# Attention products with the values in pairs of groups, four buffers of probabilities, score operands in three slots

## The reference

```python
q = x @ Wq.T + bq;  k, v = jnp.split(x @ Wkv.T + bkv, 2, axis=-1)
dots = jnp.einsum('bhid,bhjd->bhij', q * scale, k)
dots = jnp.where(causal, MASK_VAL, dots)
attn = jax.nn.softmax(dots, axis=-1)
out = jnp.einsum('bhij,bhjd->bhid', attn, v)
...
x = x + 0.5 * _L0_ffn_ref(_layernorm(x), ...)
x = x + _L0_attn_ref(_layernorm(x), ...)
x = x + 0.5 * _L0_ffn_ref(_layernorm(x), ...)
```

## Time and profile before

| | us |
|---|---|
| median of 3 runs | 1394.63 (1393.09 to 1396.85) |
| the profiled execution, its own time | 1394.48 |
| its span in the trace | 1392.7 |
| TensorE busy | 1265.0 |
| VectorE busy | 1095.3 |
| ScalarE busy | 941.5 |
| GpSimd busy | 397.6 |

### The profile page before, as it was taken

How to read it: one execution, slowest core, us unless ns; L and a number is a source line. 1 busy time by engine, 2 the same in 40 slices (tenths; PEclk the granted TensorE clock), 3 DMA queues, 4 the chain that set the end, 5 groups by cost and what they waited for, 6 DMA issues and landing times.

```text
span 1392.7 us, 24439 instructions
## 1 busy us (share of the span) xinstructions
PE 1265.0 (91%) x8356; PEld 547.7 (39%) x8356; DVE 1095.3 (79%) x3527; ACT 941.5 (68%) x1697; POOL 397.6 (29%) x508
## 2 busy tenths in 40 slices
PE   3879999999999999999999999999999999998973
PEld 2323334443344433443344433444344533433332
DVE  5788888778888888878887788878888788779643
ACT  2257776777767677767767777676777677666661
POOL 3223322332323322232323232233223323221120
PEclk9899999999999999999999999999999999999897
DMA  4480433542425433244435423154342234330000
GB/s 139 90 169 13 69 69 57 99 86 56 72 36 99 89 68 69 47 80 84 69 58 99 97 53 71 28 99 96 61 69 56 51 73 69 68 58 31 1 16 19
DMA packets 57832, 95.17 MB, mean 68 GB/s; under 512 B 8352, under 2 KB 51488, under 8 KB 51744
## 3 DMA queue, kind: packets, MB, share of 16 engines
q1 hardware_dynamic: 55664, 92.30, 35.1%
q10 hardware_dynamic: 2032, 1.19, 0.3%
HBM read 59.91 MB, written 33.55 MB: 67 GB/s over the span
## 4 chain that ended last, share of the span: by engine, by line
PE 59%; DVE 17%; ACT 12%; issue 5%; POOL 3%; DVEq 2%; DMA 2%; SPq 1%; POOLq 0%; ACTq 0%
PE o_bank L1225 15%; PE s L1206 13%; PE st L1191 11%; PE misc L1141 7%; ACT q_stack L796 5%; DVE s L953 5%; ACT probs L809 5%; PE misc L1167 4%; PE misc L1136 4%; DVE max_full L957 3%; PE misc L497 3%; POOL probs L682 1%; DVE o_tok L1043 1%; DVE stats L464 1%; PE misc L488 1%
## 5 line engine op out<-in xcount | busy, mean ns | idle before, releaser
L809 ACT ACTIVATE probs<-st 128x512 f32<-128x512 f32 (+1 forms) x1216 | 633.3, 582 | 199.8 <-PE st L1191 109.2
L953 DVE CUSTOM_DVE_ANT_0 s<-s,causal 128x128 f32<-128x128 f32 (+3 forms) x1024 | 494.8, 502 | 140.9 <-PE s L1206 138.1
L1206 PE MATMUL s<-k_stack,q_stack 96*128 96x512 bf16 (+3 forms) x1536 | 490.9, 332 | 38.3 <-DVE max_full L957 12.2
L1191 PE MATMUL st<-q_stack,k_stack 108*128 108x512 bf16 (+3 forms) x1536 | 485.7, 329 | 24.2 <-ACT probs L809 21.6
L957 DVE TENSOR_REDUCE max_full<-s 128x1 f32<-128x512 f32 x512 | 350.0, 684 | 30.8 <-PE s L1206 29.4
L1225 PE MATMUL o_bank<-probs,v_aug 128*17 128x512 f32 (+3 forms) x3072 | 325.7, 496 | 8.8 <-POOL probs L682 6.5
L682 POOL TENSOR_SCALAR_AFFINE_SELECT probs<-probs 128x512 f32<-128x512 f32 x256 | 163.7, 644 | 535.0 <-ACT probs L809 534.8
L1206 PEld LDWEIGHTS s<-k_stack,q_stack 96*128 96x128 bf16 x1536 | 148.9, 98 | 394.8 <-DVE max_diag L953 178.1
L1191 PEld LDWEIGHTS st<-q_stack,k_stack 108*128 108x128 bf16 x1536 | 149.3, 98 | 145.3 <-ACT probs L809 54.9
L694 POOL TENSOR_TENSOR qk<-qk,parts 128x512 f32<-128x512 f32 x64 | 74.2, 1159 | 318.4 <-ACT parts L769 318.4
L953 DVE DVE_READ_ACCUMULATOR2_ANT max_diag<- 128x1 f32 x1024 | 144.8, 141 | 0.0
(11 more groups left out here) (107 smaller groups left out, 859.9 us busy)
## 6 DMA issues: line engine op xcount, KB each, us to landing
part_dram<-parts SPq DMA_DIRECT2D x128, 192.0 KB, 2.8
k_stack<-part_dram SPq DMA_DIRECT2D x186, 128.0 KB, 7.0
q_stack<-part_dram SPq DMA_DIRECT2D x31, 384.0 KB, 5.0
x_all<-x SPq DMA_DIRECT2D x16, 512.0 KB, 10.6
q_stack<-part_dram SPq DMA_DIRECT2D x31, 256.0 KB, 7.4
out<-x_all SPq DMA_DIRECT2D x7, 1024.0 KB, 11.1
q_stack<-part_dram SPq DMA_DIRECT2D x33, 128.0 KB, 8.8
k_stack<-part_dram SPq DMA_DIRECT2D x12, 64.0 KB, 2.9
```

Of the source, the lines that this page charges most:

```text
L809: nc.scalar.activation(probs[:, g % 2, h - part:h + 1, 0:width], st_bank[i % 3][:, 0:share * width] .rearrange("p (h c) -> p h c", c=width ...
L953: nc.vector.tensor_tensor_reduce(out=bank, in0=bank, in1=causal[:, CW - width:CW], scale=1.0, scalar=-BIG, op0=ALU.add, op1=ALU.max, accum ...
L1191: score = nc.tensor.matmul(st_bank[i % 3][:, part * width:(part + 1) * width], k_stack[0:KROWS + MROWS, hg, h, jb * P:(jb + 1) * P], q_sta ...
L1206: nc.tensor.matmul(s_bank[u % 3][:, 0:width], q_stack[0:KROWS, hm, h, ib * P:(ib + 1) * P], k_stack[0:KROWS, hm, h, j0:j0 + width], start= ...
```

## The change

- `pv` no longer stands behind the first `st` of every group, but behind the third `st` of every odd group, two at a time: groups `g-3` and `g-2` (`PV_AT = 2`). `oev` moves to the second unit of groups 2 and 6 (`OEV_AT = 1`).
- `probs` has four buffers in place of two (`PBUF = 4`), and the exponential's wait becomes one for the `pv` of group `g-4`.
- `q_stack` and `k_stack` have three slots in place of four (`SLOTS = 3`); a step uses slot `step % 3`. Their 9 DMAs are issued by an event of its own, `stack`, at unit 1 of the step two ahead of the one that reads them with `st`, once all `st` of the step before have run (`st_full`).
- The table `PLACE` has other units for most jobs.
- The first part of the program fills the constant rows of three slots in place of four.

```diff
 PLACE = {
-    "v": (5, 9, 18, 21), "otr3": (1, 12), "qk3": (15, 24), "x_norm": (8, 24), "xt": (27, 30, 38, 44),
...
+    "v": (8, 16, 24, 40), "otr3": (1, 13), "qk3": (0, 32), "x_norm": (8, 24), "xt": (26, 30, 38, 44),
...
-OEV_AT = 0
+PV_AT, OEV_AT = 2, 1
...
+    if hg == 1 or (prev if hg == 0 else nxt):
+        put(PLACE["stack"], ("stack", (hg + 2) % NG))
...
-            if h == 0 and not (hg == 0 and not prev and g < 2):
-
-                plan.append(("pv", (g - 2) % NGRP))
-            if h == OEV_AT and g in (1, CT + 1) and not (hg == 0 and not prev and g == 1):
-                plan.append(("oev", int(g == 1)))
+            if h == PV_AT and g % 2 == 1 and not (hg == 0 and not prev and g == 1):
+                plan += [("pv", (g - 3) % NGRP), ("pv", (g - 2) % NGRP)]
+            if h == OEV_AT and g in (2, CT + 2) and not (hg == 0 and not prev and g == 2):
+                plan.append(("oev", int(g == 2)))
...
-        q_stack = sb("q_stack", [P, NG, HG, S], BF16)
-        k_stack = sb("k_stack", [P, NG, HG, S], BF16)
+        q_stack = sb("q_stack", [P, SLOTS, HG, S], BF16)
+        k_stack = sb("k_stack", [P, SLOTS, HG, S], BF16)
...
-        probs = sb("probs", [P, 2, HG, CW])
+        probs = sb("probs", [P, PBUF, HG, CW])
...
+            def load_stack(sig, step):
+
+                hq, at = step % NG, slot(step)
+                for half in range(2):
+                    eng.wait_ge(sig.parts_out[half], 32 * (step + 1))
+                wait(eng, sig.st_full, NSB * (step - SLOTS + 1))
...
+                elif kind == "stack":
+                    load_stack(sig, NG * b + hg + 2)
...
-                        wait(eng, sig.pv_done, lin(b, NGRP * NG, NGRP * hg + g - 1))
+                        wait(eng, sig.pv_done, lin(b, NGRP * NG, NGRP * hg + g - PBUF + 1))
```

More of the change, by code:

```diff
@@ L46 @@
 VW = HD + 1
+SLOTS = 3
+PBUF = 4
 BIG = 3.0e38
@@ L58 @@
 PLACE = {
[5 rows of a table removed]
[4 rows of a table added]
+    "stack": 1, "end": (27, 28, 30, 32, 34), "top2": 17, "before": ((12, 17), (12, 28)), "xload": 0, "top0": (2, 4), "count0": 2,
     "total0": 7, "pro_v": (1, 3), "pro_qk": (8, 17, 26, 35, 44, 53), "pro_before": (5, 12),
@@ L118, with slot @@
 MAX_UNITS = max_units()
+def slot(step):
+    return step % SLOTS
 HALF_UNITS = (CT * HG, NU)
@@ L568, in moe_sync @@
                 moe_experts(eng, layer, None, None, expert)
+            def load_stack(sig, step):
[3 more added lines that the diff above has]
+                wait(eng, sig.st_full, NSB * (step - SLOTS + 1))
+                for r, times, part in RUNS:
+                    rows = slice(r * HD, (r + times) * HD)
+                    eng.dma_start(q_stack[rows, at, :, :].rearrange("r h c -> r (h c)"),
+                                  part_dram[hq, 0, 0:times, :, :].rearrange("k (d h) c -> (k d) (h c)", h=HG))\
+                       .then_inc(sig.stack_in[hq], 16)
+                    for copy in range(times):
+                        rows = slice((r + copy) * HD, (r + copy + 1) * HD)
+                        eng.dma_start(k_stack[rows, at, :, :].rearrange("r h c -> r (h c)"),
+                                      part_dram[hq, 1, part, :, :].rearrange("(d h) c -> d (h c)", h=HG))\
+                           .then_inc(sig.stack_in[hq], 16)
             def handle(sig, b, n, hg, kind, *a):
@@ L1198, in handle @@
                     ahead, u = a
-                    hm = (hg + ahead) % NG
+                    hm, at = (hg + ahead) % NG, slot(NG * b + hg + ahead)
                     ib, h, j0, width, _ = MAX_UNITS[u]
@@ L1205, in handle @@
                     wait(eng, sig.max_done, lin(b, NU * NG, NU * (hg + ahead) + u - 2))
-                    nc.tensor.matmul(s_bank[u % 3][:, 0:width], q_stack[0:KROWS, hm, h, ib * P:(ib + 1) * P],
-                                     k_stack[0:KROWS, hm, h, j0:j0 + width], start=True, stop=True)\
+                    nc.tensor.matmul(s_bank[u % 3][:, 0:width], q_stack[0:KROWS, at, h, ib * P:(ib + 1) * P],
+                                     k_stack[0:KROWS, at, h, j0:j0 + width], start=True, stop=True)\
                         .then_inc(sig.s_full, 1)
@@ L1226, in handle @@
                                                 v_aug[:, jb, of % NG * HG + h, :],
-                                                probs[:, g % 2, h, 0:CW - off], start=g in (0, CT),
+                                                probs[:, g % PBUF, h, 0:CW - off], start=g in (0, CT),
                                                 stop=g in (CT - 1, NGRP - 1))
```

37 lines of the change are left out of this document (12 added, 25 removed), and 7 rows, old and new, of the table PLACE.

## The result

The change takes 1569.49 us (median of 4 runs, 1565.65 to 1576.61) against 1394.02 us for the kernel before (4 runs): 1.1266 times the time, 95% interval 1.1248 to 1.1284. It is slower by 175 us; 1368 had been forecast. The span is 1563.9 us.

A forecast was written before the change was run, and what follows sets the result against it. TensorE, busy 91%, was taken as the bound. Per inner batch 4.6 + 0.9 + 1.8 - 4.0 = 3.3 us saved, 20 over six, plus 2 and 3 for first and last: 25 off 1394.5, say 1368; range 1340 to 1394.

The forecast's parts named there:

- Joins: Paired `pv` on TensorE save switches into and out of strips: 24 joins at 0.21 us, 5.0 us a batch, 4.6 net.
- The rival without a join: The second `pv` does not enter behind the first without a break: 1404 us, slower; chance 0.04.
- Waits for masking: Later `pv` no longer waits for GpSimd's masking: 0.9 us a batch saved.
- Loads at nothing: Stack DMAs issued at unit 1 land well before the first `s` reads them at unit 33: no cost.
- Buffers: ScalarE's exponentials never wait for `pv` again, so `st` waits less for banks: 1.8 us a batch saved, ends 0 and 3.5.
- Turns: New table makes TensorE wait for `misc` to be emptied: 5.8 us a batch at full price, 4.0 taken.
- turns absorbed: Rival: waits for `misc` fall where TensorE would have stopped for VectorE or ScalarE anyway: 1341 us; chance 0.20.
- Bursts at nothing: A 512-column pair holds TensorE 1.9 us; VectorE's three banks cover 2.0 us, just enough: no cost.
- The starved rival: VectorE idles behind heavy jobs two units after a pair; at 0.4 us each, 5.6 a batch, 1409 us; chance 0.08.
- The clock: TensorE's clock is granted in full in all four steps of the inner batch, so it has no part.
- The marks set for it: Profile signs: 512-wide pairs 1.8 to 1.9 us, no `o_bank` wait, idle before jobs, steps 2 and 3 1 to 1.5 shorter.

The follow-up runs named there:

- e4: Kernel before with four buffers of probabilities and three stack slots loaded at unit 1; products, `oev` and table as before: 1389.42 us, ratio 0.9968.
- early pairs: e4 with no job moved, but two products together behind the first `st` of each odd group: 1419.14 us, ratio 1.0185.
- the lightened two: e4 and the early pairs, each with VectorE's maxima taken over the first 128 columns alone: 1362.79 and 1360.16 us.

## Why the prediction was wrong

**Where the 175 us come from.** By the ladder, each row against the one ahead:

| step | median, us | difference |
|---|---|---|
| before | 1394.0 | |
| four buffers, three slots | 1389.4 | -4.6 |
| jobs shifted for the late product | 1418.7 | +29.3 |
| product late, `oev` behind it | 1424.1 | +5.4 |
| pairs, `oev` one unit into the next group | 1494.9 | +70.8 |
| the rest of the new table | 1569.5 | +74.6 |

The parts are not independent: the table costs 124 us without pairs, some of it at neighbours of its own, and 75 behind them; the pairs cost 30 us early and 71 late. The turns of the second row are gone again in the third, and waits for ScalarE have come in their place.

For an inner batch the forecast was -3.3 us, and +24.2 were measured. Term by term:

**Joins: right.** 5.0 us a batch gross were forecast, 5.7 measured. At full clock a visit to the strips costs 0.10 us going in and 0.13 coming out (medians of 377 single products before), a pair of products 0.10 and 0.14 once (173 in the change). The rival without a join fell. The Trainium skill's page "TensorEngine Tiling (Array Packing)", section "Key Properties", says that a change of tiling mode drains TensorE. Priced at 0.35 us a join, as the prediction tried it, this would have made the kernel 27 us faster still; 24 joins saved 0.24 us each here.

**Waits for masking: right in kind, somewhat small.** 0.9 forecast, 1.4 measured (1.4 before, none after). **Loads at nothing: right**: e4 lost nothing, and the waits of `s` for `k_stack` are two, 10.1 us over the run, where they were 10.5.

**Buffers: too large.** 1.8 us a batch forecast, 0.5 measured for buffers and slots together. The step read `st`'s weight loads as waiting for exponentials that the buffers delay; the account of starts has 4.0 us a batch of such waits before and 3.9 with four buffers.

**Turns: this step failed, and not in the prices.** It set them at 4.0 us a batch net, 5.8 at full price, and they rose by 9.6. The single prices held in the change: 1.26 forecast for `otr` at 1 and `mtr` at 33, 1.27 and 1.42 measured; 0.8 and 0.99 for `ont`; 0.8 and 0.91 for `mtr` at 40; 1.1 and 1.20 for `mtr` at 42; 2.0 and 1.87 for `qk` at 40 (0.72 and 0.97 in kernels without pairs). Two things were wrong. The list was short: `otr` at 13 was set at 0.3 us and waits 0.77; `lt` and `xg`, three and four units behind the `mtr` of 14 that the pair delays, were not on it and wait 0.98 and 0.68 in step 2, where they waited 0.32 and 0.14 (`xg` waits 0.68 with the new table alone, too); with the table alone it is `mtr` behind `otr`, 1.35 twice a batch. And the reasoning that took 4.0 of the full 5.8 ("VectorE and ScalarE have banks full when TensorE stops") had the wrong sign. In none of four kernels was a turn absorbed. Between the `mtr` one `qk` cost 2.1 us a batch for 1.8 of turns, the shifts 3.8 for 2.2, the first `qk` at 8 cost 3.6 for 2.5, the eight `qk` 11.1 for 7.2: 1.2 to 1.7 times the wait itself. What the surplus is made of is not shown by a run of its own. The traces show sequences like this one of the change, step 0: behind `qk` at 0 and the wait of `otr` at 1 VectorE runs dry, and TensorE waits for VectorE 4 us later (timeline of both engines). A cast of 1.18 us on VectorE lies in between, so not all of the last wait comes from the stop.

```profile
1178.37 0.69 DVE L972 TENSOR_REDUCE max_full<-s 128x1 f32<-128x512 f32 x1 [0.81 <-PE s L1220]
1179.43 0.66 PE L1175 MATMUL misc<-ident,o_raw 128*128 128x128 f32 x4 [1.10 <-ACT parts L784]
1180.12 0.26 DVE L1055 RECIPROCAL sum_inv<-misc 128x16 f32<-128x16 f32 x1 [1.07 <-PE misc L1175]
...
1184.19 0.39 PE L1220 MATMUL s<-k_stack,q_stack 96*128 96x512 bf16 x1 [1.07 <-DVE max_diag L968]
```

The rival "turns absorbed" (1341, 0.20) fell with it.

**Bursts at nothing: this step failed.** "Just covered" asked whether three banks, 2.0 us of VectorE's work, outlast a pair of 1.9 us. The cost lies elsewhere, between the pairs. By the step's own prices VectorE needs 0.66 us a unit, and TensorE 0.44 without a product or a job; a product in every group had given VectorE time in every fourth unit, and a pair gives it in every eighth. The early pairs cost 5.9 us a batch of waits for VectorE, and these go with VectorE's load (0.4 and 0.8 us in the lightened two). The starved rival came nearest, for it let VectorE idle where TensorE is held up. But its condition, that it decides only once VectorE's share passes about 90%, was wrong: the share in the change is 36.56/52.50 = 70% in the longest step and 79% at most. VectorE idles in one stretch and is late in the next. A share cannot show that; VectorE's idle time and TensorE's waits for VectorE rise together, from 29.7 to 49.7 and from 4.0 to 12.1 us a batch. Its 1409 was 160 us too low: it counted a stall behind each heavy job and kept the turns at 4.0. Of the waits for ScalarE, +7.8 us a batch, the sum had nothing but what it put into the turns.

**The clock: this step failed.** "It has no part in the change" was read from a kernel in which TensorE hardly stopped. In the change about 10 us of each inner batch run at half clock. The columns that ran in them would have taken 4.7 us less at full clock, which is most of the +5.9 in the rest.

**The marks set for it.** Idle time of about 1 us ahead of `mtr`, `otr` and `qk` in steps 0 and 1, and none of ScalarE for `o_bank`, both came true, and so did the 512-wide pair, 1.84 us to the next start at full clock. Steps 0 and 1 were to take 43 and 42.5 us and take 52.5 and 46.9. Steps 2 and 3 were to be 1 to 1.5 us shorter and are 5.6 and 3.8 longer; the mark for the starved case, waits for `s` well above before's, holds (222.7 against 138.1 us).

**What stays open.** Why a late single product makes `st` wait for ScalarE (4.2 us a batch), and what ScalarE's waits in the change would fall to with a lighter ScalarE. Why the pairs cost 71 us late and 30 early: the account puts 2 of the 8 us a batch on the rest, where half clock is 5.7 us a batch against 0.6, and the `oev` was moved with them. And whether the stretch at a step's start, in which VectorE sets the pace, hides heavy jobs.

## What to carry to other kernels

When several engines are each below 90% and tied by rings of two or three banks, judge a burst or a stop unit by unit: whether the ring covers the burst, and also whether the consumer keeps up in the stretch that the burst's work was taken from. Take every wait that is added in full, and in this kernel up to two thirds more, never as absorbed, unless an experiment shows it. A wait that vanishes from a list of waits is worth only what the sum over all releasers of that instruction loses. Of a new table of places, list for each shared bank every two neighbours, and what stands between them; here two neighbours in a step cost about what the step's six joins gained (1.35 against 1.4 us) before any wait that followed from it.

## What the runs showed of the hardware

TensorE's granted clock fell to half (1.2 of 2.4 GHz) in the middle of the kernel, which before did not show between 90.1 and 1288.0 us. Windows ahead of such a fall, in it and behind it, the same columns as above:

```profile
1211.90:1215.30 3.40, 1.64 (x13) 0.66 (x15) 2.87 (x15) 3.38 (x5) 1.14 (x2) 1.00 0.02 5
1215.30:1218.70 3.40, 3.40 (x19) 0.81 (x12) 1.29 (x4) 0.62 (x2) 1.31 (x2) 0.54 0.22 45
1218.70:1222.10 3.40, 3.10 (x16) 2.16 (x14) 1.33 (x6) 1.00 (x3) 0.64 (x1) 0.96 0.25 70
```

TensorE had been busy for 1.64 of 3.40 us, behind `mtr` (1.26 us of idle time ahead of it, for the `qk` of unit 32) and with 1.72 us of idle time for ScalarE. The pair that follows pays for it:

```profile
1214.34 0.34 PE L1205 MATMUL st<-q_stack,k_stack 108*128 108x384 bf16 x1 [1.72 <-ACT probs L824]
...
1215.10 3.20 PE L1239 MATMUL o_bank<-probs,v_aug 128*17 128x512 f32 x16
1218.23 0.40 PE L1220 MATMUL s<-k_stack,q_stack 96*128 96x256 bf16 x1
```

It takes 3.13 us to the next start, where the same pair at full clock takes 1.84. The kernel with the change's `qk` places stops for up to 1.4 us at a time, 10.8 us of turns a batch, twice within 3.3 us at units 40 and 42 of step 1, with no half clock in its inner batches; what decides is not worked out here. The other kernels with pairs show 0.6 to 16 us of it a batch, those with single products none to 6.8, and e4 none.
